# A tower kernel's output stage: sixteen tiles instead of nine are gated while the last chunk is solved

## The reference

```python
out = dplr_delta_rule(q, k, v, a, gk).reshape(b, n, d)     # a recurrence over the 38 tokens, per head
gate = jax.nn.sigmoid(x @ Wg1 @ Wg2)
out = out * gate
mu = jnp.mean(out, axis=-1, keepdims=True)
var = jnp.mean(jnp.square(out - mu), axis=-1, keepdims=True)
out = (out - mu) * jax.lax.rsqrt(var + 1e-05) * norm_w
return out @ Wo
```

## Time and profile before

| | us |
|---|---|
| median of three runs | 1787.33 |
| the profiled execution | 1785.2 |
| its span, first to last instruction | 1783.4 |
| `output_tail`, first to last instruction | 1610.8 to 1702.5 |
| the feed-forward stage behind it | 1703.2 to the end |

### The profile page before, as it was taken

The page is one execution under the profiler, slowest core; times in us unless marked ns, Lnnn a source line. Parts: engine busy times, 40 slices in busy tenths (PEclk is TensorE's granted clock), DMA queues, the critical chain, the costliest instruction groups (busy, mean ns, idle before and its releaser), DMA issues. The chain is left out here.

```text
span 1783.4 us, 49082 instructions
## 1 busy us (share of the span) xinstructions
PE 1640.2 (92%) x21601; PEld 1474.9 (83%) x21601; DVE 1084.7 (61%) x2399; ACT 688.6 (39%) x1451; POOL 334.1 (19%) x331
## 2 busy tenths in 40 slices
PE   8889978999999999999999999977899999878789
PEld 8778856898888999999999999956788888767568
DVE  7677757655555554555546455554667676664985
ACT  6566644232222222322323222264343444333642
POOL 4633336000000000000000000034332323200840
PEclk9899969999999999999999999987676676665989
DMA  6000011000000010000001000010000000001001
GB/s 218 1 2 3 2 51 48 1 25 24 1 24 24 2 47 1 24 25 24 24 1 48 1 1 1 1 39 2 2 4 4 4 4 4 4 4 53 1 13 45
DMA packets 11844, 36.09 MB, mean 20 GB/s; under 512 B 3416, under 2 KB 8048, under 8 KB 9200
## 3 DMA queue, kind: packets, MB, share of 16 engines
q1 hardware_dynamic: 11632, 32.97, 5.4%
HBM read 30.47 MB, written 2.49 MB: 18 GB/s over the span
## 5 line engine op out<-in xcount | busy, mean ns | idle before, releaser
L1038 ACT ACTIVATE hidden<-bank,moe_b 128x512 f32<-128x512 f32 (+1 forms) x320 | 213.3, 668 | 536.9 <-PE bank L930 524.7
L947 PE MATMUL bank<-moe_w2h,hidden_hi 128*128 128x256 f32 x1216 | 345.7, 284 | 0.0
L947 PE MATMUL bank<-moe_w2l,hidden_hi 128*128 128x256 f32 x1216 | 344.0, 283 | 0.0
L947 PE MATMUL bank<-moe_w2h,hidden_lo 128*128 128x256 f32 x1216 | 344.0, 283 | 0.0
L1072 DVE SCALAR_TENSOR_TENSOR residual<-bank,gates,residual 128x256 f32<-128x256 f32 x152 | 73.4, 483 | 290.5 <-PE bank L947 290.5
L930 PE MATMUL bank<-x_hi,moe_w1h 128*128 128x512 f32 (+1 forms) x640 | 244.3, 382 | 1.9 <-ACT hidden L1038 1.9
L930 PE MATMUL bank<-x_lo,moe_w1h 128*128 128x512 f32 (+1 forms) x640 | 243.0, 380 | 0.0
L930 PE MATMUL bank<-x_hi,moe_w1l 128*128 128x512 f32 (+1 forms) x640 | 242.5, 379 | 0.0
L947 PEld LDWEIGHTS bank<-moe_w2h,hidden_hi 128*128 128x128 f32 x1216 | 233.1, 192 | 5.9 <-DVE residual L1072 4.3
L947 PEld LDWEIGHTS bank<-moe_w2l,hidden_hi 128*128 128x128 f32 x1216 | 233.2, 192 | 1.2
L947 PEld LDWEIGHTS bank<-moe_w2h,hidden_lo 128*128 128x128 f32 x1216 | 233.2, 192 | 0.0
(11 more groups left out here) (334 smaller groups left out, 3214.7 us busy)
## 6 DMA issues: line engine op xcount, KB each, us to landing
moe_w<-in_moe_w SPq DMA_DIRECT2D x16, 1024.0 KB, 4.8
patches<-in_patches SPq DMA_DIRECT2D x7, 864.0 KB, 5.7
out<-residual SPq DMA_DIRECT2D x19, 128.0 KB, 1.7
ffn_w<-in_ffn_w SPq DMA_DIRECT2D x2, 1024.0 KB, 6.4
att_w<-in_att_w SPq DMA_DIRECT2D x1, 1536.0 KB, 9.6
patches<-in_patches SPq DMA_DIRECT2D x6, 144.0 KB, 3.1
tok_w<-in_tok_w SPq DMA_DIRECT2D x6, 128.0 KB, 2.7
qk_and_ak<-in_delta_w SPq DMA_DIRECT2D x1, 768.0 KB
```

The lines of the kernel that those rows point to most:

```text
L947: mm = nc.tensor.matmul(bank[4 + n % 3][:, 0:D], left, right, start=(i == 0), stop=(i == len(passes) - 1))
L1038: nc.scalar.activation(H[:, i % 4, 0:n], bank[i % 4][:, 0:n], ACT.Relu, bias=b1[:, x, f:f + 1]).then_inc(acted, 1)
```

## The change

`LEAD`, the number of tiles that are gated while the last chunk is solved, goes from 9 to 16, all that don't need the last chunk. The three groups of deviations (tiles 0 to 8, 9 to 13, 14 to 18) become two (0 to 15, 16 to 18). The tiles are spread over the solving part: on PE the two halves' pieces stand ahead of tiles 0, 2, 5, 7, 9, 11, 13 and 14, on DVE and ACT the order is changed to match. In the loop tiles 16, 17 and 18 are gated in the rounds in which they were before (`ROWS_AHEAD` = 9: rounds 7 to 9). ACT's `odd_out` and DVE's `whole_out` now stand ahead of the first group's deviations and inverses. No computation is added or dropped.

The diff, with the rounds' guards (`if j + ROWS_AHEAD >= LEAD`) shown once:

```diff
@@ -1270,9 +1270,10 @@
         ternary_ffn(nc, sb, bank, RES, XH, XL, out, w1t, w2t, b1, b2)
 
 
-LEAD = 9
+LEAD = 16
+ROWS_AHEAD = 9
 PARTS = HALVES * FF // D
-GROUPS = (range(0, LEAD), range(LEAD, 14), range(14, TILES))
+GROUPS = (range(0, LEAD), range(LEAD, TILES))
 
 
 def output_tail(nc, bank, ins, RES, BN, MV, STD, XN, XH, XL, ident, identr, G1, wg2s, woh, wol,
@@ -1314,7 +1315,7 @@
             return bank[4 + t % 2][:, 0:D]
 
         def row_bank(t):
-            return bank[6 + t % 2 if t <= LEAD else t % 2]
+            return bank[6 + t % 2 if t < LEAD else t % 2]
 
         def half(n):
             return slice(n * PAD, (n + 1) * PAD)
@@ -1352,7 +1353,7 @@
                     return
                 if t >= 2:
                     pe.wait_ge(y_ready, t - 1)
-                if t == LEAD + 1:
+                if t == LEAD:
                     pe.wait_ge(o_whole, 4)
                 if t * P + P > y * CT:
                     pe.wait_ge(o_lo, 4)
@@ -1377,7 +1378,7 @@
             def project(t):
                 pe.wait_ge(lo_1, t + 1)
                 if t < 2:
-                    pe.wait_ge(y_ready, LEAD + t)
+                    pe.wait_ge(y_ready, LEAD)
                 else:
                     pe.wait_ge(summed, t - 1)
                 passes = [x for k in range(HALVES) for x in split_products(
@@ -1449,28 +1450,18 @@
                 gate(2 * t + 1)
                 token_rows(t)
 
-            first_half(0)
-            gates_and_rows(0)
-            first_half(1)
-            gates_and_rows(1)
-            gates_and_rows(2)
-            remainder(0)
-            gates_and_rows(3)
-            remainder(1)
-            gates_and_rows(4)
-            gates_and_rows(5)
-            second_half(0)
-            gates_and_rows(6)
-            second_half(1)
-            gates_and_rows(7)
-            gates_and_rows(8)
-            gate(2 * LEAD)
-            output(0)
-            output(1)
+            solve = {0: (first_half, 0), 2: (first_half, 1), 5: (remainder, 0), 7: (remainder, 1), 9: (second_half, 0),
+                     11: (second_half, 1), 13: (output, 0), 14: (output, 1)}
+            for t in range(LEAD):
+                if t in solve:
+                    work, i = solve[t]
+                    work(i)
+                gates_and_rows(t)
             for j in range(TILES + 3):
                 if j < TILES:
                     turn_gated(j)
-                token_rows(j + LEAD)
+                if j + ROWS_AHEAD >= LEAD:
+                    token_rows(j + ROWS_AHEAD)
                 if 0 <= j - 1 < TILES:
                     project(j - 1)
                 if j == 2:
@@ -1538,20 +1529,18 @@
                 nc.scalar.activation(out_view(xh_c, i, n), OW[:, i, n], ACT.Copy).then_inc(o_hi, 1)
 
             first_back(0)
-            gates(0, 1)
+            gates(*range(4))
             first_back(1)
-            gates(*range(2, 12))
+            gates(*range(4, 18))
             solution(0)
-            gates(12, 13)
+            gates(18)
             solution(1)
-            gates(*range(14, TILES))
             act.wait_ge(eps_set, 1)
+            for i in range(2):
+                odd_out(i, 0)
+                odd_out(i, 1)
             deviations(0)
-            odd_out(0, 0)
-            odd_out(0, 1)
             norm_gated(0)
-            odd_out(1, 0)
-            odd_out(1, 1)
             for j in range(TILES + 3):
                 if j == 1:
                     for i in range(2):
@@ -1561,8 +1550,8 @@
                     deviation(j - 3)
                 if j < TILES:
                     high_gated(j)
-                if j in (6, 11):
-                    deviations(1 if j == 6 else 2)
+                if j == 11:
+                    deviations(1)
                 if j + 1 < TILES:
                     norm_gated(j + 1)
                 if 0 <= j - 3 < TILES:
@@ -1670,23 +1659,27 @@
                 nc.vector.tensor_scalar(S[:, 2, :], S[:, 1, :], 0.5, None, ALU.mult).then_inc(cut, 1)
                 nc.vector.tensor_scalar(S[:, 3, :], S[:, 1, :], -0.5, None, ALU.mult).then_inc(cut, 1)
 
-            for t in range(3):
+            for t in range(5):
                 measured(t)
             with_values(0)
-            measured(3)
+            measured(5)
+            measured(6)
             with_values(1)
-            for t in range(4, 7):
-                measured(t)
-            magnitude(0)
             measured(7)
             measured(8)
+            magnitude(0)
+            for t in range(9, 14):
+                measured(t)
+            whole_out(0, 0)
+            whole_out(0, 1)
+            measured(14)
+            whole_out(1, 0)
+            whole_out(1, 1)
+            measured(15)
             gated_stats(LEAD - 1)
             gated_aggregate(LEAD - 2)
             gated_aggregate(LEAD - 1)
             inverses(0)
-            for i in range(2):
-                whole_out(i, 0)
-                whole_out(i, 1)
             magnitude(1)
             for j in range(TILES + 5):
                 if 0 <= j - 1 < TILES:
@@ -1699,19 +1692,22 @@
                     scales()
                 if 0 <= j - 3 < TILES:
                     inverse(j - 3)
-                gated(j + LEAD)
+                if j + ROWS_AHEAD >= LEAD:
+                    gated(j + ROWS_AHEAD)
...
```

More of the change, by code:

```diff
@@ L1706, in _ @@
                     add(j - 2)
-                gated_stats(j + LEAD)
+                if j + ROWS_AHEAD >= LEAD:
+                    gated_stats(j + ROWS_AHEAD)
                 if 0 <= j - 2 < TILES:
                     sum_stats(j - 2)
-                gated_aggregate(j + LEAD)
+                if j + ROWS_AHEAD >= LEAD:
+                    gated_aggregate(j + ROWS_AHEAD)
                 if 0 <= j - 2 < TILES:
                     sum_aggregate(j - 2)
-                if j in (6, 11):
-                    inverses(1 if j == 6 else 2)
+                if j == 11:
+                    inverses(1)
         @block.gpsimd
```

## The result

The changed kernel takes 1790.76 us (median of 18 runs, 1786.62 to 1794.77) against 1787.15 for the kernel before on the same chip (18 runs). The ratio is 1.0023, 95% interval 1.0015 to 1.0032: about 4.1 us slower, between 2.7 and 5.7 (the medians alone lie 3.6 apart). The forecast was 1792.0. The profiled execution took 1790.53 us, 5.3 more than that of before. 1.5 of these lie ahead of the stage, in code that the change doesn't touch. The stage itself, from PE's first instruction to DVE's last, took 95.51 us against 91.70: +3.81. What follows the stage took 80.9 us in both.

A forecast was written before the change was run, and what follows sets the result against it. PE at half clock was taken to bound the solving part, POOL to pace the loop. Terms: +6.2 + 0.8 + 2.5 - 4.1 = +5.4, less 0.8 for the clock, +4.6: 1792.0 us, range 1787.0 to 1794.2.

The forecast's parts named there:

- seven tiles' rows, with the clock: PE in the solving part: 28 more row matmuls cost +6.2 us, a short full-clock stretch gives back 0.8.
- wait before tile 15's product: End of the solving part: tile 15's product waits on DVE behind two whole_out, 0.8 us, bounds 0 to 1.5.
- chain to the first transposition: From tile 15's product to PE's first transposition: 4.19 us, now all bare, +2.5 net of PE's earlier 1.65 idle.
- transposition to POOL's start: Between solving part and loop: DVE has less queued before the scales, 5.6 us instead of 9.7, so -4.1.
- loop and its end: From POOL's start to the last x_lo: 50.05 us as before since POOL paces it, 0, bounds -3.5 and +0.5.
- So no wait of the solve gets longer: Solving part: the solve's returns on ACT and DVE get more tiles in front, counted as nothing, up to -0.8 us.
- the run that was to raise it: PE, solving part: tiles 2, 3, 4 back to back for 4.4 us were expected to bring a full-clock stretch, -0.8 us.
- rival B: Loop: minus_mean slips past w_ternary, so eight to ten rounds take 2.35 us instead of 2.69; 1788.8 us, chance 0.10.
- The signs: Events that would show the forecast right: first transposition at 1651 to 1653 us, scales about 1657.5, last x_lo at 1707.
- Rival A: PE's solving part: the clock rises early and stays, over two thirds of the part at full clock; 1785.6 us, chance 0.08.
- in-between: PE's solving part: a third of it at full clock, +2.5 us, 1789.8 us; chance 0.17.
- rival C: Seven tiles ride in idle time of the solving part and the loop is 5.3 us shorter; 1783.5 us, chance 0.05.

The follow-up runs named there:

- a_load_late: Changed kernel with ACT's wait for eps moved back to directly ahead of deviations(0); one execution took 1794.18 us, stage 96.75 us.
- a_one_input: Changed kernel with POOL's two-input subtraction for the ternary weights replaced by a one-input operation; timed 1.0010 against the kernel before, stage 92.16 us.
- a_scales_early: Changed kernel with both magnitudes, the sum over partitions and the scales made in the solving part; timed 1.0012 against the kernel before, stage 93.93 us.
- b_load_early: Kernel before with ACT's wait for eps moved to the head of its list; stage 90.55 us against 91.70, first transposition 31.20 against 31.94.
- b_one_input: Kernel before with POOL's two-input subtraction for the ternary weights replaced by a one-input operation; timed 0.9986, stage 89.14 us against 91.70.
- a_lead_12: Changed kernel with twelve tiles instead of sixteen gated in the solving part, groups 0 to 11 and 12 to 18; timed 1.0010 against the kernel before.

## Why the prediction was right, step by step

| step | forecast | measured |
|---|---|---|
| seven tiles' rows, with the clock | +6.2 - 0.8 | +5.27 |
| wait before tile 15's product | 0.8 | 0.9 |
| chain to the first transposition (1.65 of it PE idled before) | 4.2, +2.5 net | 2.89; with the wait +2.12 net |
| transposition to POOL's start | -4.1 | -3.69 |
| loop and its end | 0 | +0.11 |
| sum | +4.6 | +3.81 in the trace, +4.1 timed |

*The rows* were right in their sum and partly wrong inside it. The rows cost 6.2 and PE's old idle time of about 0.8 went, the most that was allowed for. But a new wait of 0.91 us came at 1617.06: the bank of the next gates is free only when ACT has taken the two before, and these stand behind the sigmoid's table load:

```profile
1615.32 1.28 ACT L1511 ACT_TABLE_LOAD   x1
1616.62 0.66 ACT L1511 ACTIVATE gate_then_gated<-bank 128x256 f32<-128x256 f32 x2
```

"So no wait of the solve gets longer" had looked at the solve's own returns and not at what now starts earlier on ACT. The clock gave back about 0.9 us, against 0.8, but not where I had reasoned it: the stretch of tiles 2 to 4, the run that was to raise it, 4.04 us long, stayed at 0.50. It rose around the end of the second outputs, for the rows of tiles 14 and 15:

```profile
1620.83:1624.87 4.04, 4.04 (x24) 3.92 (x19) 1.68 (x6) 2.48 (x7) 0.00 (x0) 0.50 0.01 4
...
1646.00:1648.00 2.00, 1.91 (x68) 1.64 (x48) 1.64 (x7) 1.01 (x3) 0.00 (x0) 0.84 0.00 0
```

And not in every execution: three variants with nearly the same PE work up to there (`a_load_late`, `a_one_input`, `a_scales_early`) ended the solving part at 36.48, 36.50 and 36.92. So +5.27 is one of two outcomes, the other being +6.2 to +6.6. What decides between them stays open, and that the clock's 0.8 came out in this trace is luck, as is that the new wait of 0.91 was about cancelled by the 0.9. The Trainium skill's page TensorE: Matmul & The Clock Gate, part 1 (What's actually happening), has activity release the clock. By that rule alone this part would have run at full clock; with PE busy for 34.64 of its 35.70 us it was granted 0.52.

*The wait before tile 15's product* was sized well.

*The chain* is the term that was mis-sized: 2.89 in place of 4.19. I took the table load as part of the chain, because the earlier trace rows has it behind the aggregate. `a_load_late` and `b_load_early` show that it was there by the place of another wait. The other traces with the same order of work bear it out: from the last product to the first transposition it is 4.19, 4.18 (`b_one_input`) and 4.23 (`a_load_late`) with the load behind the aggregate, 2.89, 2.88 (`a_one_input`) and 2.89 (`a_scales_early`) with it well ahead, and 3.46 in `b_load_early`, where it starts only behind the last sigmoid. The diff showed the odd outputs coming between that wait and `deviations(0)`, and I read past it. Wait and chain together brought +2.12 where 3.3 were forecast; less the 0.4 that the next step fell short, this is the distance between +4.6 and +3.81.

*Transposition to POOL's start*: 6.02 us against 5.6 counted. DVE idled 0.96 us before the second `x_lo` where I had put 0.7.

*The loop*: right, and for the reason given. POOL paces it by holding `minus_mean`; replacing the subtraction by an operation of one input freed 1.9 us of it in the kernel before and 4.0 in the changed one, and moving POOL's work out ahead freed the rounds behind its end. Part of what the lighter DVE saved, it gave back in being held, 1.9 us in `minus_mean` alone. So rival B's event did not occur, though its mechanism is real. The 5.3 us that the loop was said to lose were 3.0 behind POOL's start: the prediction counted tiles 9 to 11 in the step ahead of it as well. As the loop's term was 0, the sum doesn't feel it. One reading of it was wrong: the 0.17 us inside `is_up` were taken to show that a POOL instruction with one input doesn't hold `minus_mean`. It does (see the last section), and what gave B a chance was only that this hold is shorter.

*The signs* came at the times named (first transposition at 1651.68, POOL at 1657.70, the last `w_ternary` at 1700.10, the last `x_lo` at 1707.44), but 1.5 us of each lie ahead of the stage. Counted from the stage's start, with the clock's 0.8 taken off, the first transposition came at 39.33 where the working had 40.7, and POOL at 45.35 where it had 46.3. PE idled for 3.78 us where over 4 were named. This follows from the mis-sized chain. Beside POOL the `std` stood 2.67 apart on average, but between 2.34 and 2.91 and not evenly at 2.69: now and then a `minus_mean` starts late enough in its round to be held for only a part of `w_ternary`.

*Rival A* fell with the clock of 0.52 (its in-between, a third of the part at full clock, was priced at +2.5; a third of its own 7 us leaves about +3), *rival C* with the full PE. `a_lead_12` shows C wrong from the other side: four tiles fewer ahead make the stage 3.0 us shorter.

*Groups*: not tested by themselves. The two groups held up nobody in the changed kernel.

## What to carry to other kernels

Work that is moved ahead pays only if the engine it lands on is free there and the place it leaves is what paces: here PE had 1 us free and got 6.2, and the loop, which lost 3.0 us of DVE's work beside POOL, was held by POOL. Ask first which single instruction is held, and by what; moving the holder's work away was worth more than moving the held engine's. When an activation waits for two things, look at which of them its table load carries, and fulfil the old one earlier in the queue.

## What was not expected of the hardware

How long POOL holds DVE depended on POOL's instruction. A DVE instruction on one column with two tensors took 0.16 us alone. Started inside POOL's subtraction of two tensors it ended with it in every case, after up to 0.74 us. Started 0.1 to 0.3 us into a POOL instruction with one tensor (and at most a threshold for each partition) it was held as well, but only up to 0.44 or 0.45 us ahead of that one's end; started later it took 0.16. The kernel before has such a case too:

```profile
1671.27 0.93 POOL L1724 TENSOR_SCALAR is_up<-ffn_w,scales 128x256 f32<-128x256 f32 x1
...
1671.51 0.24 DVE L1624 SCALAR_TENSOR_TENSOR minus_mean<-mean_var,std 128x1 f32<-128x1 f32 x1
```

It ends at 1671.75, 0.45 us ahead of `is_up`; the one at 1668.91 ends 0.44 us ahead of its `is_up`, so its 0.17 us show no freedom from the hold. In `a_one_input` it is up to 0.39 us, with a median of 0.16. The Trainium skill's page SBUF — State Buffer (Who interferes with whom) has such an instruction contend with any GpSimd instruction that reads SBUF. These traces agree with it.

A table load costs its 1.28 us and no more here: in `b_load_early` it starts at 1639.82 and `std` at 1641.12, 0.02 us behind its end, and in the changed kernel nothing of it is on the chain.
